# Spread of the pooling weights in 32x32 TensorE tiles in place of 64x128, in a recommender attention kernel

## The reference

```python
outer = jnp.einsum('bi,bnj->bnij', candidate_ad, goods).reshape(Bs, Ns, Ks * Ks)
k_b = jnp.broadcast_to(candidate_ad[:, None, :], (Bs, Ns, Ks))
h1 = jnp.concatenate((k_b, goods, outer), axis=-1)
act = jax.nn.sigmoid(h1 @ W1 + b1)
weight = act @ W2 + b2
out = jnp.sum(goods * weight, axis=1)
```

## Time and profile before

| what | value |
|---|---|
| median of 3 runs | 262.45 us (262.2 to 263.8) |
| the profiled execution, its own time | 262.6 us |
| its span, first to last instruction | 260.8 us |
| instructions | 18353 |
| PE, PEld busy | 248.3 us (95%), 133.6 us (51%) |
| DVE, ACT, POOL busy | 209.6 us (80%), 224.3 us (86%), 147.0 us (56%) |
| mean granted clock of TensorE | 0.992 of full speed |

### The profile page before, as it was taken

The page is one execution under the profiler, slowest core; times in us unless marked ns, Lnnn a source line. Parts: engine busy times, 40 slices in busy tenths (PEclk is TensorE's granted clock), DMA queues, the critical chain, the costliest instruction groups (busy, mean ns, idle before and its releaser), DMA issues.

```text
span 260.8 us, 18353 instructions
## 1 busy us (share of the span) xinstructions
PE 248.3 (95%) x7492; PEld 133.6 (51%) x7492; DVE 209.6 (80%) x1176; ACT 224.3 (86%) x658; POOL 147.0 (56%) x285
## 2 busy tenths in 40 slices
PE   6997989999999999999999999999999999999970
PEld 2335545455555555555555555555555555555540
DVE  0892568679888889888888888898888898888896
ACT  2898978978999999999999999999999999999940
POOL 1300664646766566665666666656666566665562
PEclk9999999999999999999999999999999999999996
DMA  5991876767778787777778887877777877887100
GB/s 209 284 322 29 248 221 181 224 189 232 242 225 239 224 225 237 234 238 227 223 221 244 227 249 207 239 232 240 229 233 224 230 237 233 238 230 224 53 1 10
DMA packets 38243, 55.10 MB, mean 211 GB/s; under 512 B 4256, under 2 KB 37920, under 8 KB 38048
## 3 DMA queue, kind: packets, MB, share of 16 engines
q1 hardware_dynamic: 37920, 54.41, 70.5%
q10 hardware_dynamic: 288, 0.32, 0.3%
HBM read 54.45 MB, written 0.26 MB: 210 GB/s over the span
## 4 chain that ended last, share of the span: by engine, by line
PE 87%; ACT 7%; DVE 2%; DMA 2%; issue 1%; ACTq 0%; DVEq 0%
PE w_ps L394 28%; PE z_ps L349 25%; PE x_ps L370 16%; PE w_ps L430 6%; PE x_ps L430 6%; PE s_ps L349 4%; ACT wm L485 4%; DMA act<-w_outer 2%; DVE goods L557 2%; ACT act L506 2%; ACT wxd L485 1%; PE z_ps L300 0%; ACT actx L514 0%; DVE whole L550 0%; PE z_ps L430 0%
## 5 line engine op out<-in xcount | busy, mean ns | idle before, releaser
L506 ACT ACTIVATE act<-z_ps,bias 128x200 f32<-128x200 f32 x384 | 129.4, 440 | 20.5 <-PE z_ps L349 10.9
L349 PE MATMUL z_ps<-goods,wm_ring 32*32 32x200 f32 x3072 | 80.3, 340 | 2.6 <-issue 1.2
L268 POOL TENSOR_TENSOR rest<-whole,top 128x200 f32<-128x200 f32 x64 | 36.3, 567 | 59.5 <-DVE top L552 35.9
L557 DVE CUSTOM_DVE_ANT_0 goods<-w_ps,goods 128x200 f32<-128x200 f32 x122 | 39.8, 364 | 30.8 <-PE z_ps L430 16.0
L394 PE MATMUL w_ps<-act,consts 128*32 128x200 f32 x1024 | 56.6, 339 | 0.7 <-ACT actx L514 0.7
L370 PE MATMUL x_ps<-goods,wx 128*32 128x200 f32 x1024 | 55.4, 333 | 0.0
L270 POOL TENSOR_SCALAR mid<-rest,consts 128x200 bf16<-128x200 f32 x64 | 50.3, 785 | 6.3
L349 PEld LDWEIGHTS z_ps<-goods,wm_ring 32*32 32x32 f32 x3072 | 30.3, 103 | 34.4 <-issue 33.0
L557 DVE CUSTOM_DVE_ANT_0 goods<-z_ps,goods 128x200 f32<-128x200 f32 x140 | 44.9, 361 | 0.0
L506 ACT ACTIVATE act<-s_ps,bias 128x200 f32<-128x200 f32 x128 | 44.9, 461 | 0.0
L246 POOL COPY wx<-wxd 32x96 f32<-32x96 f32 (+1 forms) x88 | 22.8, 259 | 37.0 <-PE x_ps L370 22.8
(11 more groups left out here) (45 smaller groups left out, 233.1 us busy)
## 6 DMA issues: line engine op xcount, KB each, us to landing
goods<-goods_t SPq DMA_DIRECT2D x256, 200.0 KB, 2.8
act<-cand_r SPq DMA_DIRECT2D x1, 1024.0 KB, 5.4
act<-cand_u SPq DMA_DIRECT2D x1, 256.0 KB, 3.0
candb<-cand_b SPq DMA_DIRECT2D x1, 256.0 KB, 3.8
out_t<-out_stage SPq DMA_DIRECT2D x4, 64.0 KB, 3.1
consts<-small ACTq DMA_DIRECT2D x1, 164.5 KB, 5.4
act<-w_outer ACTq DMA_DIRECT2D x1, 144.0 KB, 5.6
pick_sb<-pick SPq DMA_DIRECT2D x1, 128.0 KB, 3.5
```

Of the source, the lines that this page charges most:

```text
L268: nc.gpsimd.tensor_tensor(rest[:, :], whole[:, q % 2, :], top[:, q % 2, :], ALU.subtract).then_inc(part_step, 1)
L349: last = nc.tensor.matmul(z_bank(slot, r)[32 * c:32 * c + 32, N * s:N * s + N], wm_ring[32 * r:32 * r + 32, slot % RING, 4 * s + c, :], go ...
L506: last = nc.scalar.activation(act[:, p % A_SLOTS, r, N * s:N * s + N], z_bank(p, r)[:, N * s:N * s + N], ACT.Sigmoid, bias=bias[:, r, p, s ...
L557: one = nc.vector.tensor_tensor_reduce(goods[:, q % G_SLOTS, v, :], s_banks(q, f)[s][:, N * i:N * i + N], goods[:, q % G_SLOTS, v, :], 1.0 ...
```

## The change

`spread` uses 32x32 tiles. Rows 64s to 64s+63 of the stack are taken as two strips of 32; for each unit and half, four matmuls make the four strips of 32 output partitions, the first two from the lower row strip and the other two from the upper. A call so has 16 matmuls in place of 4. The waits around it move: products s=0 waits for pooled[0][1] at its start, and for pooled[1][1] ahead of r=3 in place of r=2; each spread call has a wait for pick_loaded in front.

```diff
@@ products
                         pe.wait_ge(z_read, p)
+                    if slot >= LAG + 1:
+
+                        pe.wait_ge(pooled[0][1], p)
                 for r in range(4):
-                    if s == 0 and r == 2 and slot >= LAG + 1:
+                    if s == 0 and r == 3 and slot >= LAG + 1:
 
                         pe.wait_ge(pick_loaded, 16)
-                        pe.wait_ge(pooled[0][1], p)
                         pe.wait_ge(pooled[1][1], p)
@@ spread
                 q = slot - LAG
+                pe.wait_ge(pick_loaded, 16)
                 if f == 0:
                     pe.wait_ge(stack_made, p)
...
                 for i in range(2):
                     for s in range(2):
-                        rows = slice(64 * s, 64 * s + 64)
-                        last = nc.tensor.matmul(s_banks(q, f)[s][:, N * i:N * i + N], pick_sb[rows, 2 * f + i, :],
-                                                stack[rows, q % 2, :], start=True, stop=True)
+                        for r in range(4):
+
+                            rows = slice(64 * s + 32 * (r // 2), 64 * s + 32 * (r // 2) + 32)
+                            last = nc.tensor.matmul(s_banks(q, f)[s][32 * r:32 * r + 32, N * i:N * i + N],
+                                                    pick_sb[rows, 2 * f + i, 32 * r:32 * r + 32],
+                                                    stack[rows, q % 2, :], start=True, stop=True)
                 last.then_inc(s_done, 1)
```

## The result

Median of six runs of the changed kernel: 265.09 us (263.48 to 266.11), of six runs of the kernel before: 262.32; ratio 1.009 (1.0057 to 1.0124). Timed again later, ten runs against 23: 264.17 against 262.14, ratio 1.0061 (1.0031 to 1.009). Forecast was 257.2, faster; it became slower by somewhat less than 1%. The profiled execution took 263.48 (span 261.7), 0.88 more than that of before.

What follows compares the result with a forecast made beforehand. It took a slot loop through spread f=0, two DVE units, row sums and products as the bound. From 262.6 us, 6.0 less (60 x 0.10) and 0.8 more for code gave 257.4, median 257.2; range 252.0 to 266.0.

Steps and rivals of the forecast that it cites:

- Step 1: Products s=0 to spread f=0: the tile shape no longer changes, so the drain of about 0.09 us goes.
- Rival B: Products to spread: the drain stays and spread starts at 0.63 as now; 263.3 to 265.7 us, chance 0.14.
- rival A: Spread: row strips take turns at a PSUM bank, 0.18 us a turn; 282 us, chance 0.10.
- Step 2: Products s=0: moving the pooled[1][1] wait to r=3 gains the last strip nothing; its last matmul stays at 0.37 us.
- Step 3: Spread f=0: 16 matmuls cost no time of their own; last starts at 0.63, DVE 0.10 us earlier (0.07 to 0.17).
- Step 4: Around products s=1 and spread f=1: two more drains go, worth nothing; about 0.3 us idle before row sums.
- Step 5: Spread calls and products s=0: one added wait each costs nothing; uncovered they are 0.24 us a slot.
- rival E: Spread calls and products s=0: the added waits are uncovered, 0.24 us a slot; 271.6 us, chance 0.06.
- Step 6: Loop's first pass: 357 more PE instructions are 1.4 code transfers, +0.8 us (0 to 1.5).
- Step 7: Tail of three pairs: bound by GpSimd's stack and DVE, so no change.
- Rival D: Loop: it no longer fits PE's code store, nine passes pay about 4 us each; 293 us, chance 0.05.

Runs made afterwards that it cites:

- e4: The changed kernel with both waits of products s=0 put back in front of r=2; 263.78 us, ratio 1.0068.
- e1: The changed kernel with spread f=1 left in the old 64x128 tiles, only f=0 in 32x32; 264.49 us, ratio 1.0074.
- e8: The kernel before with 32x32 tiles only for spread f=0 in the loop's slots; 260.65 us, ratio 0.9921; again 260.87 us, ratio 0.9956.
- e2: The kernel before with spread f=1 in 32x32 tiles, f=0 and the waits of the products as before; 270.38 us, ratio 1.0318.
- e3: The kernel before with 24 one-column matmuls and their loads ahead of row sums in each slot with a spread; 274.26 us, ratio 1.0457.
- e13: e8 with 13 one-column matmuls and their loads, 26 instructions, put ahead of the pairs; 263.38 us.
- e10: e8 with the loop's spread f=1 in small tiles too; 392.42 us, ratio 1.496.
- e5: The changed kernel with the stack and the pick matrix in f32 in place of bf16; 439.42 us.
- e11: e10 with 26 one-column matmuls and their loads, 52 instructions, put ahead of the pairs; 263.95 us.
- e7: The changed kernel with each goods transfer from the seventh pair on cut to 32 columns in place of 400; 262.87 us.

## Why the prediction was wrong

- Step 1 (the drain behind products s=0 goes): right. First spread at 0.434, against 0.632. Rival B is out. Strips in one bank start 0.0085 apart, not 0.18: rival A is out. The Trainium skill's page "TensorEngine Tiling (Array Packing)", section "Gotcha 1: PSUM Pressure", says that different row tiles cannot access the same PSUM bank simultaneously; here it did not cost a turn, and two row strips that write different partitions of one bank ran beside each other.
- Step 2 (the moved wait gains nothing): right, shown by e4. Its size was not: the last product of s=0 starts at 0.397 (0.372 before and in e4), not "as before", but the second spread matmul is at 0.55 either way.
- Step 3 ("Sixteen matmuls in place of four cost no time of their own"): mis-sized. The last one starts at 0.694, not 0.63, so the gain was 0.045 at DVE and 0.049 a slot where I had 0.10, below my lower end of 0.07. The matmuls start 0.0085 apart, and behind the first is a hold-up of 0.12 (0.17 for f=1) that nothing in the trace of before showed. It ends at P + 0.55 in every profile with small tiles for f=0 and a loop that stays. Not order, not format; its cause is open. It goes with a full array: in the tail, behind idle time, they start 0.003 apart.
- Step 4 (f=1's drains are worth nothing): right. Last spread to row sums is 0.288 for 0.176, and e1 and e8 have the same slot with f=1 in the old tiles. The three drains that went would have been worth 0.27 a slot. e2 says more: where DVE does not cover them, the small tiles of f=1 cost 0.06.
- Step 5 (added waits cost nothing): right. The slot is as expected from the last spread alone; rival E is out.
- Step 6 (code, +0.8): the step that failed by most. The loss between first and tenth row sums rose from 2.7 to 6.4 in one profile and 7.8 in the other, 3.7 to 5.0 for 357 instructions, 10 to 14 ns each. I had priced it at the first pass's average, 3.3 us for five to six transfers. But that average is over code that nearly came in time. Before, 1378 instructions in six slots are about one block of 256 in 3.98 us; after, 1684 are one in 3.2 us. The transfers of the first pass, before from 34 to 57 us and changed from 34 to 60:
```profile
q8 instruction: 6, 0.10, 2.0%
```
```profile
q8 instruction: 7, 0.11, 1.8%
```
By their records the six start from 35.3 to 56.3, the seven from 34.7 to 59.7: 4.2 apart in both kernels. My reading: the instructions needed per us outgrew what came, and each further one costs up to its whole delivery, 4.2 us / 256 = 16 ns by this estimate. The runs bear it out in size only roughly, and not as a mechanism: e3 without the tiles has 10 ns for each of 336, e8 8 ns for each of 150, and e1 19 for each of 182, which is above that bound; e1 and e8 differ by six instructions in the loop, and e13 shows that place accounts for much of it. The clock that falls behind a long stop, in three of the profiles, is inside these losses and not on top of them; I had not thought of it. My worst end, 1.5, was that of 1.4 transfers landing late, not of PE outrunning all of them.
- Step 7 (tail): right within 0.15.
- Rival D (the loop no longer fits) did not happen to this kernel, but e10 and e5 are it, at 392 and 439 where I had 293. I treated fitting as a matter of length; e10 against e11 shows that it isn't.

With measured terms the profiled pair adds up: +0.26, +3.21 (which holds 9 x 0.05 of gain), -2.72, +0.15 = +0.9.

Neither error turns the sign alone. In the prediction's own sum, -6.0 with 3.7 to 5.0 for the code is still -2.3 to -1.0, and -2.9 (60 x 0.049) with 0.8 is -2.1; both together give +0.8 to +2.1. That the measured 265.09 lies in the range, and in rival B's 263.3 to 265.7, is luck: B's drain was gone.

The Trainium skill's page "Runtime: NRT & Kernel Launch", section "Instruction fetch mechanics", gives PE an instruction memory of 2048 instructions, refilled in blocks of 256, and says that crossing a block mostly costs nothing that is seen. The traces agree with the block (9 transfers for 2325 instructions) and with e5, whose 2068 never stay. They disagree on the cost here, where a first pass needs a block in 3.2 us and gets one in 4.2, and the 1678 of e10 show that less than 2048 can miss as well.

What stays open: the cause of the 0.12; the places that a loop may have; and how the loss of the changed kernel divides between length and place (the kernel before does not mind being moved, e8 minds).

## What to carry to other kernels

Price added instructions on a full engine by how fast its code arrives against how fast it is used, not by an average stall: a loop that gains 0.05 a slot has to run long to pay back a first pass at 10 to 14 ns an instruction (8 to 19 over the kernels here). Change only the part whose end another engine waits for, and only in the loop that repeats; here this was worth 0.4 to 0.8% where the whole change lost 0.6 to 0.9%. When a loop comes near the size of the code store, look at code transfers in its later passes and try it a few instructions further on.

## What the hardware showed beyond that

- A kernel with a loop of 1678 PE instructions took 392 us or 264 us for a shift by 52 instructions; a loop of 1684 stayed at both of its places.
- With a shift by 26, e8 took 1.6 us more from first to tenth row sums (one profile, so not clear of its spread) and 0.1 more in every later pass, without one more code transfer (12 in both).
- A PE stop of 1.63 us at 2.4 GHz was followed, 0.6 us after its end, by 3.4 us at 1.2 GHz; stops of 1.58 (e4), 1.64 (e11) and 1.72 (e7) were not. What decides there is open.
- bf16 matmuls on 32x32 tiles behind f32 products start mostly 0.0085 apart after a 0.12 hold-up, and products behind them without a drain 0.017 apart where 0.006 to 0.007 is usual.
